# A graph kernel's prologue: raw projection by chunks, node bounds by products, scaling on ScalarE and bias on GpSimd

## The reference, cut to what matters

```python
x = x + _L0_gnn_ref(_layernorm(x, axis=-1), edge_index, W, att_src, att_dst, bias, gamma, beta)
# inside:
xh = (x @ W).reshape(N, H, D)
a_src = jnp.einsum('nhd,hd->nh', xh, att_src)
a_dst = jnp.einsum('nhd,hd->nh', xh, att_dst)
e = jax.nn.leaky_relu(a_src[src] + a_dst[dst], NEG_SLOPE)
...
out = jax.ops.segment_sum(msg, dst, num_segments=N).reshape(N, H * D) + bias
```

## Time and profile before

| | us |
|---|---|
| median of 3 runs | 1978.06 |
| lowest, highest | 1973.62, 1979.04 |
| the profiled execution, its span | 1977.53, 1975.8 |
| TensorE busy (share of the span) | 1365.6 (69%) |
| GpSimd busy | 1098.3 (56%) |
| VectorE busy | 907.3 (46%) |
| ScalarE busy | 576.3 (29%) |
| first block | 0 to 100.7 |
| second block | 100.7 to 163.4 |

### The profile page before, as it was taken

How to read it: one execution, slowest core, us unless ns; L and a number is a source line. 1 busy time by engine, 2 the same in 40 slices (tenths; PEclk the granted TensorE clock), 3 DMA queues, 4 the chain that set the end, 5 groups by cost and what they waited for, 6 DMA issues and landing times. The chain is left out here.

```text
span 1975.8 us, 23808 instructions
## 1 busy us (share of the span) xinstructions
PE 1365.6 (69%) x6688; PEld 1134.1 (57%) x6688; DVE 907.3 (46%) x1818; ACT 576.3 (29%) x1264; POOL 1098.3 (56%) x1086
## 2 busy tenths in 40 slices
PE   2435666656666266599999997656666666567998
PEld 2324544444454146599999997444445444346787
DVE  7425544444443667633333333644334333335953
ACT  2133433323333014133333332422222222222310
POOL 4477777777774600377222273077777777773520
PEclk7756878878878575699999999877878787978999
DMA  6484998888887601432111122743333333330002
GB/s 145 119 251 150 298 312 284 281 285 272 276 283 258 155 6 63 134 115 83 46 46 46 46 98 65 174 142 104 105 105 105 105 104 105 106 99 1 1 1 65
DMA packets 156809, 268.56 MB, mean 136 GB/s; under 512 B 26747, under 2 KB 119839, under 8 KB 155567
## 3 DMA queue, kind: packets, MB, share of 16 engines
q1 hardware_dynamic: 100252, 135.75, 22.1%
q0 software_dynamic: 46224, 123.97, 21.0%
q10 hardware_dynamic: 10213, 7.36, 1.5%
HBM read 169.82 MB, written 98.15 MB: 136 GB/s over the span
## 5 line engine op out<-in xcount | busy, mean ns | idle before, releaser
L1182 POOL DMA_INDIRECT sum_rows<-xn_tab,src_e x391 | 373.3, 955 | 174.5 <-issue 118.8
L1207 PE MATMUL bank<-sum_held,sum_hot 128*125 128x256 f32 x976 | 304.1, 474 | 195.3 <-ACT sum_held L1217 191.1
L798 POOL DMA_INDIRECT gat_rows<-xh_tab,src_e x363 | 343.4, 946 | 114.8 <-issue 107.8
L1207 PEld LDWEIGHTS bank<-sum_held,sum_hot 128*125 128x125 f32 x976 | 222.2, 236 | 273.5 <-issue 179.7
L871 PE MATMUL bank<-gat_rows,gat_same 128*128 128x264 f32 x784 | 263.7, 483 | 126.2 <-issue 126.2
L871 PEld LDWEIGHTS bank<-gat_rows,gat_same 128*128 128x128 f32 x784 | 176.6, 244 | 166.4 <-issue 132.6
L1217 ACT COPY sum_held<-sum_rows 128x1024 f32 x122 | 127.4, 1045 | 373.6 <-SPq L1173 334.1
L1894 PE MATMUL bank<-weights,e_xthigh 128*128 x896 | 220.3, 330 | 8.5 <-DVE e_xtlow L2049 5.4
L915 ACT COPY gat_outs<-bank 128x528 f32<-128x528 f32 x196 | 117.3, 598 | 281.8 <-PE bank L871 280.5
L2054 DVE TENSOR_TENSOR e_h<-e_gated,bank 128x342 f32<-128x342 f32 x112 | 57.1, 510 | 262.9 <-ACT e_gated L1987 262.9
L1239 DVE SCALAR_TENSOR_TENSOR res<-bank,prep_inv,res 125x256 f32 x122 | 58.9, 483 | 234.8 <-PE bank L1207 228.2
(11 more groups left out here) (508 smaller groups left out, 2416.8 us busy)
## 6 DMA issues: line engine op xcount, KB each, us to landing
parts<-gat_outs SPq DMA_DIRECT2D x27, 1904.0 KB, 8.0
staged<-w_tab SPq DMA_DIRECT2D x8, 2132.0 KB, 8.9
w_tab<-w_stage SPq DMA_DIRECT2D x16, 682.0 KB, 10.6
w_raw<-in_L_ffn_w_dram SPq DMA_DIRECT2D x16, 640.0 KB
gat_rows<-xh_tab,src_e POOLq DMA_INDIRECT x391, 4.7
sum_rows<-xn_tab,src_e POOLq DMA_INDIRECT x391, 2.8
w_tab<-w_stage SPq DMA_DIRECT2D x8, 768.0 KB, 10.6
weights<-y_tab SPq DMA_DIRECT2D x10, 600.0 KB
```

Source lines behind the costliest of these rows:

```text
L798: pool.indirect_dma_start(out=rows[b % R][:, t, :], out_offset=None, in_=k.xh_tab, in_offset=bass.IndirectOffsetOnAxis(ap=k.src_e[:, b * S ...
L1182: pool.indirect_dma_start(out=rows[:, at // IP % (RING * GPAIRS), at % IP, :], out_offset=None, in_=k.xn_tab, in_offset=bass.IndirectOffse ...
L1207: m = nc.tensor.matmul(k.ps[s][0:P, 0:C], hot[g % 2][:, s, c, :], held[:, s, c, :], start=(c == 0), stop=(c == IP - 1))
```

## The change

- **Loads.** x comes in five chunks with a semaphore each, issued right behind the edge loads; W and the attention vectors no longer wait for the edges. The last edge tile of the partition before is loaded once more (`prev_i`). `dst_pad` and `start_tab` are gone with their DMAs.
- **Projection.** TensorE transposes raw x and multiplies by a W from which the mean of each column was taken (a product with `ones`, then two operations on VectorE), so the mean of x drops out. ScalarE scales by 1/deviation as it reads the product out of the bank, GpSimd adds the bias. Transposes of tile t and the product of tile t - 1 alternate. VectorE only takes statistics and reciprocals, chunk by chunk. SyncE stores all rows of `xh_tab`, and the attention parts after them.
- **Node bounds.** GpSimd compares all node numbers with the first destination of each edge tile (`passed`, four times 3125 columns). TensorE multiplies `passed` by the rises of the destinations from edge tile to edge tile (`rises`, 129 columns), four products per node tile: the bank then holds for each node the edge tile in which it begins, and in column 129 that tile's number. VectorE counts three tiles of each chunk, ScalarE two; one copy per chunk keeps the tile numbers. The ends come from two products with shifted unit matrices.
- **Second block.** `joins` is made there, on 8 partitions in place of 128, and the mean of x from `stats`.

The diff's core:

```diff
-            sp.wait_ge(edges_f, 1)
-            sp.dma_start(k.dst_pad.rearrange("(q e) -> q e", q=Q), dstq[:, :]).then_inc(pad_out, 16)
-            move(sp, k.res[:, :, :], k.a["x"].rearrange("(t p) c -> p t c", p=P), x_in)
+            for c in range(CHUNKS):
+                move(sp, k.res[:, c * TB:(c + 1) * TB, :], x_rows[:, c * TB:(c + 1) * TB, :], x_in[c])
...
+            for c in range(CHUNKS):
+                tiles = slice(c * TB, (c + 1) * TB)
+                sp.wait_ge(taken, (c + 1) * TB)
+                move(sp, xh_rows[:, tiles, :], k.xh[:, tiles, 0:XW], xh_done)
...
         def _(act):
...
-            act.wait_ge(edges_in, 96)
             act.dma_start(w[:, :, 0:C], k.a["L0_gnn_W"].rearrange("(a p) c -> p a c", p=128)).then_inc(w_in, 16)
...
+            def scale(t):
+                act.wait_ge(projected, t + 1)
+                act.wait_ge(inverted, t // TB + 1)
+                nc.scalar.activation(k.xh[:, t, :], k.ps[XR + t % XP][0:P, 0:RW], ACT.Identity, scale=k.rstd[:, t:t + 1]).then_inc(scaled, 1)
...
+            for c in range(CHUNKS):
+                for t in range(c * TB + BY_DVE, (c + 1) * TB):
+                    act.wait_ge(windows, t + 1)
+                    nc.scalar.activation(trash[:, t % TB, :], k.ps[XR + t % XP][0:P, 0:EP], ACT.Sign, bias=half[:, t:t + 1], scale=-1.0,
+                                         accum_out=before[:, t:t + 1]).then_inc(signed, 1)
...
         def _(pool):
...
+            me(pool, nc.gpsimd.iota(node_row, pattern=[[1, N]], base=0, channel_multiplier=0, allow_small_or_imprecise_dtypes=True))
+            pool.wait_ge(firsts_made, 1)
+            for j in range(J):
+                nc.gpsimd.tensor_scalar(passed[:, j, :], node_row, first_dst[:, j:j + 1], None, ALU.is_gt).then_inc(passed_made, 1)
...
-                pool.indirect_dma_start(out=windows[:, t, :], out_offset=None, in_=k.dst_pad.rearrange("(a b) -> a b", b=EP),
-                                        in_offset=bass.IndirectOffsetOnAxis(ap=tiles_i[:, t:t + 1], axis=0)).then_inc(windows_in, 16)
+                pool.wait_ge(scaled, t + 1)
+                nc.gpsimd.tensor_tensor(k.xh[:, t, 0:C], k.xh[:, t, 0:C], bias[:, 0:C], ALU.add).then_inc(taken, 1)
...
         def _(pe):
...
+            for t in range(NT + 1):
+                if t < NT:
...
+                    for c in range(2):
+                        last_mm = nc.tensor.transpose(k.ps[t % XR][:, c * P:(c + 1) * P], k.res[:, t, c * 128:(c + 1) * 128], k.ident[0:P, 0:P])
                     last_mm.then_inc(xt_turned, 1)
+                if t:
+                    u = t - 1
...
+                    if u >= XP:
+                        pe.wait_ge(scaled, u - XP + 1)
                     for c in range(2):
+                        last_mm = nc.tensor.matmul(k.ps[XR + u % XP][0:P, 0:RW], xt[:, u % XR, c, :], w[:, c, :], start=(c == 0), stop=(c == 1))
                     last_mm.then_inc(projected, 1)
+            pe.wait_ge(passed_made, J)
+            pe.wait_ge(rises_made, 1)
+            pe.wait_ge(scaled, NT)
+            for t in range(NT):
+                c, s = t // TB, t % TB
+                if c:
+                    pe.wait_ge(tiles_kept, c)
...
+                for j in range(J):
+                    last_mm = nc.tensor.matmul(k.ps[XR + t % XP][0:P, 0:WIN], passed[:, j, t * P:(t + 1) * P], rises[:, j, :], start=(j == 0), stop=(j == J - 1))
+                last_mm.then_inc(windows, 1)
...
         def _(dve):
...
+            for c in range(CHUNKS):
+                for t in range(c * TB, c * TB + BY_DVE):
+                    dve.wait_ge(windows, t + 1)
+                    v.tensor_scalar(trash[:, t % TB, :], k.ps[XR + t % XP][0:P, 0:EP], k.node[:, t:t + 1], None, ALU.is_lt, ALU.add, accum_out=before[:, t:t + 1]).then_inc(counted, 1)
+                dve.wait_ge(signed, (c + 1) * (TB - BY_DVE))
+                v.tensor_copy(tile[:, c * TB:(c + 1) * TB], k.banks[0:P, XR:8, EP]).then_inc(tiles_kept, 1)
...
+        me(dve, v.memset(k.joins[0:H, 0:1], 0.0))
+        me(dve, v.tensor_copy(k.joins[0:H, 1:ET], self.bank[0:H, 0:ET - 1]))
+        me(dve, v.tensor_tensor(k.joins[0:H, 1:ET], self.bank[0:H, 1:ET], k.joins[0:H, 1:ET], ALU.is_equal))
```

More of the change, by code:

```diff
@@ L221, in first_phase @@
[L221 to L232, removed]
@@ L348, in _ @@
[L348 to L357 removed]
+            pe.wait_ge(w_whole, 1)
@@ L434, in take_body @@
-            def take_body(i):
-                for s in range(TB):
-                    dve.wait_ge(projected, i * TB + s + 1 + TB)
-                    v.tensor_tensor(tile_of(k.xh, i * TB + s), k.ps[3 + s][0:P, 0:RW], bias[:, :], ALU.add).then_inc(taken, 1)
-            norm_body(0)
-            dve.wait_ge(bias_in, 16)
-            dve.wait_ge(bias_tail, 1)
-            for i in range(NT // TB - 1):
-                norm_body(i + 1)
-                take_body(i)
-            take_body(NT // TB - 1)
@@ L446, in _ @@
-            dve.wait_ge(windows_in, 16 * NT)
-            for t in range(NT):
-                v.tensor_scalar(trash[:, t, 0:EP], window[:, t, :], k.node[:, t:t + 1], None, ALU.is_lt, ALU.add, accum_out=before[:, t:t + 1])
-            me(dve, v.memset(mark[:, :], 0.0))
-            v.scalar_tensor_tensor(out=start[:, :], in0=tile[:, :], scalar=float(EP), in1=before[:, :], op0=ALU.mult,
-                                   op1=ALU.add).then_inc(starts_ready, 1)
-            dve.wait_ge(starts_turned, 1)
@@ new lines, in _ @@
+            signs = before[:, :].rearrange("p (c s) -> p c s", s=TB)[:, :, BY_DVE:TB]
+            dve.wait_ge(tiles_kept, CHUNKS)
+            dve.wait_ge(counted, CHUNKS * BY_DVE)
+            me(dve, v.tensor_scalar(signs, signs, 0.5, 0.5 * EP, ALU.mult, ALU.add))
+            v.scalar_tensor_tensor(out=start[:, 0:NT], in0=tile[:, :], scalar=float(EP), in1=before[:, :], op0=ALU.mult, op1=ALU.add).then_inc(starts_made, 1)
+            dve.wait_ge(starts_made, 1)
+            me(dve, v.tensor_scalar(t0[:, :], start[:, 0:NT], -float(NO_ROW + 1), None, ALU.add))
@@ L465, in _ @@
+            dve.wait_ge(ends_made, 1)
+            end = k.ps[0][0:P, 0:NT]
+            v.tensor_scalar(last[:, :], end, -1.0, 0.0, ALU.add, ALU.max)
+            me(dve, v.tensor_tensor(k.deg[:, :], end, start[:, 0:NT], ALU.subtract))
+            me(dve, v.tensor_scalar(has[:, :], k.deg[:, :], 0.0, None, ALU.is_gt))
             me(dve, v.tensor_tensor(t0[:, :], t0[:, :], has[:, :], ALU.mult))
             me(dve, v.tensor_scalar(k.start_row[:, :], t0[:, :], float(NO_ROW + 1), None, ALU.add))
+            me(dve, v.scalar_tensor_tensor(out=last[:, :], in0=last[:, :], scalar=-float(NO_ROW), in1=has[:, :], op0=ALU.add, op1=ALU.mult))
@@ L469, in norm_stats @@
+            me(dve, v.tensor_scalar(k.main_row[:, :], last[:, :], float(NO_ROW), None, ALU.add))
 def norm_stats(k, dve, deviations, roots):
```

271 lines of the change are left out of this document (128 added, 143 removed).

## The result

| | before | after |
|---|---|---|
| median of 7 runs, us | 1976.13 (1973.26 to 1979.04) | 1988.6 (1985.27 to 1996.79) |
| profiled execution, its span | 1977.53, 1975.8 | 1988.51, 1986.8 |
| second stage starts on VectorE | 100.73 | 111.28 |
| third stage starts on VectorE | 163.43 | 175.64 |

The ratio is 1.0073 (95% interval 1.0053 to 1.0092): slower by 12.5 us, where I had forecast 13 to 15 us less. The stage that was to end 15 us earlier ends 10.6 us later, and the span grows by 11.0.

The account below looks back on a forecast made before the run. The first stage's chain (x, statistics, projection, rows out, 14 gathers, barrier) was taken as the bound. Its end moving from 100.7 to 85.5 gave 1977.5 - 15.2 + 0.5 = 1963 us, range 1956 to 1974.

Parts of the forecast that it names:

- Step 2: GpSimd's iota and four comparisons beside VectorE's work before the projection: 1.0 us in all, projection starting at 23.5.
- step 1: VectorE's work before the projection: edge work to 10.6, a wait of 3.5 us for att until 14.1, sum 22.5.
- step 4: GpSimd's bias adds (0.56 each) and gathers after the projection, chain ending at 83.4; comparisons taken at 2.8 us each.
- GpSimd slow: Comparisons of 10 us each delay bias adds and gathers: 7 us gained, 1971; together with W late 16 in 100.
- Step 3: Projection of 25 tiles on TensorE from raw x: 31.5 us, products ending at 55.0.
- low-clock rival: TensorE at half clock in the node bounds (1992, 6 in 100) or in the projection (1987, 2 in 100).
- Step 5: Node bounds on TensorE after the projection: 22.5 us of products and 4.0 of waits, first stage ending at 85.5.
- Step 6: Joins and one small operation moved to VectorE's second stage, edge rows' zero fill issued later: cost nothing.
- Us for us to the end: An earlier barrier at the first stage's end was taken as an equally earlier end of the kernel.

Follow-up runs that it names:

- the second kernel: The changed kernel with the four comparisons on VectorE instead of GpSimd and the node-number iota behind the edge work; 1963.73 us, 0.9913 of before.
- the first experiment: The changed kernel with each of GpSimd's four comparisons of 3125 columns cut into five of 625; 1971.96 us, 0.9953 of before.
- third: The second kernel with four write-only iotas of 98x3125 on GpSimd where the comparisons were; 1969.3 us, 0.9939 of before.
- the sixth: The second kernel with the five column copies moved from VectorE to ScalarE; 1957.77 us, 0.9892 of before.
- the fourth experiment: The kernel before with an iota and four unused comparisons added on GpSimd where the changed kernel has them; 2004.08 us, 1.0119 of before.
- the fifth: The kernel before with an iota and four unused comparisons added on GpSimd after the first gather batch, VectorE at rest; 2017.27 us (one run).
- The ninth: The changed kernel with GpSimd's four comparisons moved behind the centring of W; 1989.8 us, 1.0042 of before.

## Why the prediction was wrong

- **Step 2 failed**, and with it the forecast. I put GpSimd's work beside VectorE at 1.0 us in all, from two pairs of rows: 0.88 against 0.69, and 1.93 against 0.94. In both the other side's instructions were short (a select of 0.47, scans of 1.2), so a wait for the end of one of them fits both rows; I read them as a slower pace. What the runs show is a wait until about the end of GpSimd's instruction: 7.9, 7.7, 6.1 and 8.7 us on four instructions, over their times in the second kernel (0.43, 0.43, 0.68, 0.43), 30.4 in all. Of these 3.5 take the place of step 1's wait for att: 22.5 + 30.4 - 3.5 = 49.4, against the measured 49.64. Three of the four are a cast, a copy and a tensor_scalar, with one input. The section that I quoted (the Trainium skill, GPSIMD Engine Reference, "1. Specifications") names VectorE instructions in a 2-port mode beside those with two SBUF inputs. I took over only the second half of that and looked no further for the forms meant by the first.
- **The comparison's price in step 4** was 2.8 and is 8.2. It was taken from a cast, another form. I had written that it comes on the path above 7.2 each, as a matter of GpSimd's queue, and had named a comparison of over 7 us as a sign of being wrong. Nearly alone, that is what the first experiment shows: 90.66 against 83.33, 7.3 us. The lock with write-only instructions of 2.9 us costs 5.3 (third). Together they cost 28.0 (111.28 against 83.33), because each held instruction waits for one long one.
- **The rival "GpSimd slow"** had the right engine and the wrong path: with comparisons of 10 us it let VectorE go on and reached 1971 us.
- **Step 1** held where GpSimd is out of the way: in the second kernel VectorE had att at 13.0 (I took 14.1) and the projection started at 21.45 (22.5 before contention); in the sixth the edge work ended at 10.7 (10.6) and att came at 13.3.
- **Step 3** held: 30.6 us against 31.5. Neither low-clock rival came true: the granted clock was 0.94 over the projection and 1.00 in the bounds.
- **Step 5** held: 26.4 against 26.5, four waits of 0.75 (I took 1.0) and 0.94 per tile (0.90).
- **Step 4's bias adds** take 0.73, not 0.56, and stay hidden.
- **Step 6** put the second stage's extra work at nothing. That stage lasts 64.4 us after (175.64 - 111.28) and 63.4 in the second kernel, against 62.7 before. With its code unchanged it lasted 63.2 in the fourth experiment and 63.4 in the fifth, so about 1 us stands out in the changed kernel, and no run shows what makes it.
- **Us for us to the end** held to about 2 us: the stage's end moved by +10.6, -10.1, -17.4, -12.1 and +22.8 (the change, experiments one to four), the medians by +12.5, -8.2, -16.5, -10.9 and +23.9. The ninth, +4.9 and +9.8, is the exception.

## What to carry to other kernels

Before work is put on GpSimd beside VectorE, take the length of the longest single GpSimd instruction and charge it to every VectorE instruction with two SBUF inputs, and to every copy, cast and plain tensor_scalar from SBUF to SBUF, that can meet one; on the path that is the price, not a share. If it has to lie there, cut it into pieces (beside 20 of 1.9 us VectorE's held operations took 2.2 us more in all, where 4 of 8.2 us cost 30; GpSimd itself took 3.9 more) or leave it to VectorE, which did the same comparison in 2 us. A price for a new instruction form is not to be had from another form of the same engine.

## What the runs showed of the hardware

- A GpSimd comparison of 98x3125 in fp32 takes 8.2 us (2.62 ns per column) with VectorE at rest, an iota of the same size 2.8, and VectorE's comparison 1.8 to 2.1. That a one-input GpSimd form could be three times slower than its cast I had not expected.
- A small VectorE instruction is held like a large one: a tensor_tensor over 5 columns lasted 5.43 us instead of 0.17. In a profile it stands as a long duration with no idle time before it, so a list of waits doesn't show it; the same line's duration in another place does.
- Write-only instructions hold copy and cast too: 2.16 and 2.88 us instead of 0.43 beside iotas of 2.9.
- Of two that start close together the first went ahead: a tensor_scalar that started 0.04 us ahead of a comparison took 0.43 us, one that started 0.07 us behind it 9.18.
